# A graph network on one core: row gathers held to fourteen rows ahead of the scan

## The reference

```
xi = x @ W_pre[:Fin];  xj = x @ W_pre[Fin:]
h  = xi[dst] + xj[src] + b_pre
mean, mean_sq = segment_sum(h, dst) / deg, segment_sum(h * h, dst) / deg
std = sqrt(relu(mean_sq - mean * mean) + 1e-5)
mx, mn = segment_max(h, dst), segment_min(h, dst)
agg = concat(mean, mx, mn, std)
out = concat(x, agg, agg * log(deg + 1) / avg, agg * avg / log(deg + 1)) @ W_post + b_post
out = out @ W_lin + b_lin
```

## Time and profile before

| | |
|---|---|
| median of 3 runs | 2161.73 us (2159.77 to 2167.29) |
| the profiled execution | 2173.5 us, of which the span from first to last instruction is 2171.8 us |
| busy in that span | PE 68%, PE weight loads 48%, VectorE 66%, ScalarE 23%, GpSimd 37% |
| mean granted TensorE clock | 0.85 of full speed |
| the gather of layer 0, first to finish | 649.2 to 1302.6 us |
| the gather of layer 1, first to finish | 1413.1 to 2050.8 us |
| row gathers | 688, of 0.947 us each on GpSimd (median) |

### The profile page before, as it was taken

How to read it: one execution, slowest core, us unless ns; L and a number is a source line. 1 busy time by engine, 2 the same in 40 slices (tenths; PEclk the granted TensorE clock), 3 DMA queues, 4 the chain that set the end, 5 groups by cost and what they waited for, 6 DMA issues and landing times.

```text
span 2171.8 us, 30279 instructions
## 1 busy us (share of the span) xinstructions
PE 1475.0 (68%) x11250; PEld 1050.9 (48%) x11250; DVE 1424.4 (66%) x2879; ACT 502.8 (23%) x1074; POOL 808.6 (37%) x831
## 2 busy tenths in 40 slices
PE   0267777767964677777787774656876786687563
PEld 0167766656952445445454552424544554455432
DVE  7899999692065666556665652786755675565457
ACT  3366777300031011111111110221111111111101
POOL 4400000032006545546555514075554555545230
PEclk9878999887986888889898886978898998888877
DMA  5323333333412455455555542145554565554320
GB/s 116 91 107 151 136 137 150 127 114 123 163 63 80 157 181 179 160 177 187 173 184 185 168 152 92 43 135 167 178 172 153 195 197 162 184 168 163 134 70 24
DMA packets 126240, 309.36 MB, mean 142 GB/s; under 512 B 21745, under 2 KB 73409, under 8 KB 125743
## 3 DMA queue, kind: packets, MB, share of 16 engines
q1 hardware_dynamic: 75216, 145.00, 19.0%
q10 hardware_dynamic: 23470, 105.20, 13.9%
q0 software_dynamic: 27440, 57.77, 9.9%
HBM read 167.18 MB, written 140.75 MB: 142 GB/s over the span
## 4 chain that ended last, share of the span: by engine, by line
PE 33%; DVE 32%; another core or an unknown queue 14%; issue 12%; DMA 4%; ACT 2%; POOL 2%; ACTq 1%; DVEq 0%; POOLq 0%
PE ps L1156 16%; PE ps L1284 6%; DVE accs L2159 5%; DVE scanned L2188 3%; DVE accs L2141 3%; DVE scanned L1700 3%; DVE scanned L1697 3%; DVE scanned L1706 3%; PE ps L1296 2%; DMA A<-counts 2%; PE ps L1181 2%; PE ps L1450 1%; PE ps L1385 1%; DVE S L1673 1%
## 5 line engine op out<-in xcount | busy, mean ns | idle before, releaser
L1095 POOL DMA_INDIRECT scanned<-table,rest_idx x688 | 678.5, 986 | 763.0 <-DMA rest_history<-scanned 255.8
L1156 PE MATMUL ps<-big,A 125*128 125x128 bf16 (+1 forms) x7500 | 764.7, 258 | 83.0 <-issue 60.1
L1156 PEld LDWEIGHTS ps<-big,A 125*128 125x128 bf16 x7500 | 622.6, 103 | 226.0 <-issue 118.0
L1284 PE MATMUL ps<-S,big 126*128 126x500 bf16 (+1 forms) x1050 | 281.3, 412 | 254.1 <-DVE accs L2159 163.2
L2159 DVE TENSOR_TENSOR accs<-accs,ps 128x1000 f32<-128x1000 f32 (+1 forms) x154 | 166.9, 1084 | 391.1 <-remote 301.6
L2188 DVE SCALAR_TENSOR_TENSOR scanned<-scanned,rest_neg 128x256 f32<-128x256 f32 x688 | 332.0, 483 | 32.9 <-ACT scanned L905 5.5
L1284 PEld LDWEIGHTS ps<-S,big 126*128 126x128 bf16 x1050 | 101.9, 107 | 375.8 <-DVE accs L2159 179.5
L2141 DVE TENSOR_TENSOR accs<-accs,ps 128x1000 f32<-128x1000 f32 (+1 forms) x154 | 166.0, 1078 | 1.8 <-DVE MS L1814 1.1
L1181 PE MATMUL ps<-scanned 128*128 128x150 bf16 x1050 | 115.7, 252 | 75.6 <-DVE scanned L1706 74.5
L1113 POOL IOTA Y<- 128x784 int32 x1 | 0.8, 787 | 361.7 <-DVEq L1962 361.7
L1181 PEld LDWEIGHTS ps<-scanned 128*128 128x128 bf16 x1050 | 87.2, 132 | 92.6 <-issue 75.6
(11 more groups left out here) (384 smaller groups left out, 1421.7 us busy)
## 6 DMA issues: line engine op xcount, KB each, us to landing
rest_history<-scanned SPq DMA_DIRECT2D x172, 512.0 KB
A<-counts ACTq DMA_DIRECT2D x75, 800.0 KB
S<-picks SPq DMA_DIRECT2D x60, 640.0 KB
picks<-S ACTq DMA_DIRECT2D x25, 800.0 KB
counts<-A ACTq DMA_DIRECT2D x25, 800.0 KB
scanned<-table,rest_idx POOLq DMA_INDIRECT x688
table<-Y SPq DMA_DIRECT2D x10, 320.0 KB, 2.6
S<-picks SPq DMA_DIRECT2D x10, 160.0 KB
```

What stands on the lines that cost most here:

```text
L1095: nc.gpsimd.indirect_dma_start(out=lanes[:, r, s, 0:F], out_offset=None, in_=tables[1 + l], in_offset=bass.IndirectOffsetOnAxis(ap=rest_id ...
L1156: m = nc.tensor.matmul(acc[:, bank, 0:width], A[0:NB, slot, a, :], XS[0:NB, a, c, 0:width], start=a == 0 and c == 0, stop=a == NT - 1 and ...
L1284: m = nc.tensor.matmul(ps[:, bank + h, 0:len(blocks) * NB], XS[0:NB + 1, a, c, 0:F], pick[0:NB + 1, part % RING, 0:len(blocks), a % PART, ...
```

## The change

One constant is new, and each row's gather gets one more wait. Row `i` of a layer is asked for only when VectorE has scanned row `i - 14` of that layer; rows 0 to 13 stay without it. The waits ahead of a batch stay as they are.

```diff
 LANES_RING = 6
+ROWS_LEAD = 14
 ROUND = 1.5 * 2.0 ** 23
...
                         pool.wait_ge(main.scan_ops, BATCH * (n - LANES_RING + 1) + 1)
                     for s in range(BATCH):
                         i = k * BATCH + s
+                        if i >= ROWS_LEAD:
+                            pool.wait_ge(main.scan_ops, l * REST + i + 1 - ROWS_LEAD)
                         nc.gpsimd.indirect_dma_start(
                             out=lanes[:, r, s, 0:F], out_offset=None, in_=tables[1 + l],
                             in_offset=bass.IndirectOffsetOnAxis(ap=rest_idx[:, i:i + 1], axis=0))\
```

## The result

| | before | after |
|---|---|---|
| median | 2164.51 us (2159.77 to 2169.99) | 2095.10 us (2089.68 to 2103.08) |
| the profiled execution | 2173.5 us, span 2171.8 | 2097.7 us, span 2095.9 |

The ratio is 0.9681, with a 95% interval of 0.9639 to 0.9724: **3.2% faster**. Forecast were 2055 us and a range of 1980 to 2175. The sign and the range are right, the size is two thirds of the one forecast: 69 us for 106.

What follows compares the result with a forecast made beforehand. The prediction took VectorE's waits for TensorE's signal, kept up by long gather runs, to bound the stretches. Stalls -94, clock -18 and late rows +6 gave -106 us, so 2055 us from a median of 2161.7, range 1980 to 2175.

Steps and rivals of the forecast that it cites:

- What bounds it: Gather stretches: set by waiting; VectorE's 51 remote waits for TensorE's signal, 329.8 us, caused by long gather runs.
- (1): GpSimd's row gathers: distance ahead of the scan becomes 13 for every row, from 19 up to 22.
- (2): VectorE's stalls in the gather stretches: mean length falls from 6.5 to 4.3 us, bounds 2.6 and 6.4.
- (3): VectorE's stalls in the gather stretches: 55 for 51, 236 us against 330, so 94 us less.
- the formula behind it: Gather stretches: stall length = gathers that GpSimd may still ask for x 1.25 us + 2.6 us.
- (4): TensorE's clock: shorter stalls mostly end before it falls, 18 us less, bounds 0 and 52.
- (5): GpSimd's added wait instruction on each gather: costs 0, other bound 66 us if nothing hides it.
- (6): A batch's last row, gather to negation to scan: late rows cost 3 us a layer, 6 us more.
- Another cause: Rival, chance 0.09: TensorE stops by itself, the 51 stalls stay, time 2162 us within 6.
- More stalls: Rival, chance 0.13: GpSimd never rests long enough, 96 stalls, 413 us, +83, so 2245 us.
- break-even: Count of 4.3 us stalls in the gather stretches at which nothing is gained: 77.
- All but vanish: Rival, chance 0.08: any gap between gathers breaks a run, 12 stalls of 4 us left, about 1850 us.

Runs made afterwards that it cites:

- e10: Kernel before without row gathers after the first 24 rows of layer 0, on a chip with stalls: 1809.6 us against 2153.3, ratio 0.839.
- e2: Kernel before, row gathers after the first 24 rows bringing 128 lines of 64 bytes in place of 512: 1769.7 us against 1767.9, ratio 1.001.
- e7: Kernel after with a distance of 18 rows in place of 14: 1768.1 us, ratio 1.001 to the kernel before on that chip.
- e4: Kernel after with a distance of 10 rows in place of 14: 1888.8 us, ratio 1.069 to the kernel before on that chip.
- e12: Kernel before, a batch's second row asked for only when the batch ahead has landed: 2078.3 us against 2128.1, ratio 0.980.
- e9: Kernel before, a batch's first row asked for only when all four rows ahead have landed: 2245.9 us against 2153.3, ratio 1.041.

## Why the prediction held, and where it was off

**What bounds it: right in place, half right in kind.** VectorE's remote waits were the thing to touch, they come while gathers run, and in the stretches they are gone without the row gathers (e10). "TensorE itself is what stands still" is one half of it: TensorE does slow down with no wait shown (221 products for 642 in 40 us). The other half I missed: in the stall above the signal was due at once and came 7.5 us late, to two engines at the same moment. Which of the two brings the other is open. And one condition was missing that no row of one chip could show: of five chips, three stall and two don't.

**(1) The distance: right.** GpSimd's idle time names the scan, not the store.

**(2) and (3) Length and number: right.** 54 stalls of 4.6 us, for 55 of 4.3: 249 us against 236, and 80.8 saved against 94. The stretches are 612 and 599 us, where I had said near 590. But the formula behind it does not hold, so that the mean came out near is in part luck. I had read that stalls end 2.1 to 3.1 us after the run's last gather. So do 19 of the 26 waits over 6 us of the kernel before, but few of the shorter ones, and in the kernel after only about a quarter: its stalls end 0.0 to 2.7 us behind a gather's end. And from distance 14 to 12 they got no shorter.

**(4) Clock: the step furthest off.** I had stalls of 4.3 us end mostly before the clock falls, and took 18 us for it, on top of the waits. S less the held time is 938.8 us after and 938.6 before: outside the waits nothing came. The clock still falls, as short stretches of the kernel after behind a stall of 6.4 us show (columns as in the earlier trace rows):

```profile
941.00:945.00 4.00, 3.48 (x11) 1.61 (x12) 3.75 (x8) 0.83 (x2) 0.73 (x1) 0.50 0.00 0
946.00:950.00 4.00, 4.00 (x30) 2.93 (x29) 3.68 (x8) 0.86 (x2) 3.08 (x4) 1.00 0.74 211
```

At 0.50 TensorE does 11 products in 4 us, at 1.00 it does 30. But VectorE is busy 3.75 us of the slow four and 3.68 of the fast: TensorE's slower products were not what it waited for at this place. The same is seen over whole stretches. Those of the kernel before on chip 10:

```profile
622.00:1098.00 476.00, 422.95 (x2819) 289.63 (x2816) 401.66 (x697) 99.64 (x248) 346.75 (x343) 0.96 0.68 225
1190.00:1672.00 482.00, 421.85 (x2822) 289.05 (x2822) 405.90 (x700) 102.08 (x252) 347.77 (x344) 0.95 0.67 222
```

The clock is 0.95 to 0.96 there and 0.85 to 0.88 on the first chip, TensorE's products take 845 us in place of 947, and S less the held time is within 12 us (938.6 against 926.5 to 937.9 in e2, e7 and this run). Outside the stalls I had priced a resource where it isn't the bound.

One part stays open. "Held" takes a wait whole. By the modelled end of the lift, some 27 of the 330 us before lie ahead of that end and only 10 of the 249 after. In these TensorE was not done yet, and whether the clock or the crawl made it late, the traces don't say. So up to 17 us of the 80.8 saved may be the term that I had called clock.

**(5) The wait instruction: right, 0.** A distance of 18 adds as many waits as 14 but four for each layer, and its ratio is 1.001 (0.998 to 1.004).

**(6) Late rows: inside its bounds, priced on the wrong chain.** I had forecast 6 us with bounds of 0 to 16. On the first chip the 0.2 us above is what (4) and (6) come to together; on chip 10 the change costs 13 us, of which the profiled S shows none. ScalarE's wait for landings went from 53 to 257 us, and on the first chip it lay beside the stalls. On chip 10 no stall covers it, and at a distance of 10 it is 110 us of S. The chain that I priced, gather to negation to scan, is not the one that pays (17.0 us in e4): it is ScalarE's order, take_sums and loads behind the negation. I had named it and given it nothing.

So the sum was -94 - 18 + 6 = -106, and the profiled executions show -80.8 for the held time, +0.2 for the rest of S and +4.7 outside it, -75.9 in all. The waits gave 13 us less than forecast, and the clock 18 less as a term of its own.

**The rivals.** *Another cause* falls with e10. The Trainium skill, "SBUF — State Buffer", section "Who interferes with whom", says that DMA never contends with a compute engine. By its words the gathers could not cost TensorE's followers 330 us; the measurement decides, 344 us less without them. No trace shows an access to SBUF that waits, so the rule may be true of the ports and yet no ground for the forecast of 2162. *More stalls* didn't come: 54, far from the 77 of break-even. *All but vanish* by "any gap is enough" is refuted twice: the gaps that the change brings left 54 stalls, and those of e12 left 34.

On the pause of e9: the Trainium skill, "DMA: Bandwidth & Descriptors", section "Anatomy of one DMA — SWDGE (gpsimd) path", gives some 2.0 us fixed for one such transfer. An estimate by that page is 3 x 1.25 + 2.0, some 5.8 us for a batch, below my 5.9 to 6.3. The trace has 2.5 us from the start of the gather (741.44) to the start of the negation that waits for it (743.97), and 0.7 more to the next gather, so 7.0 for the batch; that last step neither the page nor I had in the sum.

## What to carry to other kernels

When two engines that wait for different signals of a third start at the same instant, long after the third's work for them by the profile, neither of the two waits is explained by that work; look at what else is going on, here a run of gathers from GpSimd, and at whether the third crawls with no wait shown. A change that treats such a stall is worth what the stall is worth on the chip where it was measured: repeat it on others, with the kernel before beside it, since here the same edit gives 3.2% on one chip and costs 0.8% on another. And price the wait that you add by who stands behind it in the same engine's order, not by the one that it is meant for.

## What the runs showed of the hardware that I had not expected

- The kernel before takes 2164.5, 2153.3 and 2128.1 us on three chips and 1767.9 and 1767.1 on two others, 20% less. On the first chip some 330 us of this are VectorE's waits for late signals of TensorE during row gathers, and 66 lie outside the stretches, in three places with other runs of gathers.
- On the first kind of chip VectorE waited up to 13.9 us for such a signal. On the second kind no signal was late, with over 250 gathers in one run. Why chips differ was not found.
- While 28 gathers went out on the first chip, 25 of them of 4-byte lines, TensorE did 221 products in 40 us at a granted clock of 0.61; on chip 10 it did 642 at 1.00.
- With at most four gathers in a run and pauses of 1.7 us or more between runs, no signal was held in 172 batches (e9, chip 2); with longer runs, 34 were (e12, chip 14).
- 128 lines of 64 bytes took as long as 128 lines of 512, on a chip without stalls: ratio 1.001.
- Apart from the stalls, stretches with a granted clock of 0.85 to 0.88 took at most 12 us longer in some 930 than those with 0.95 to 0.96, while VectorE's busy time was the same (812.6 against 807.6 us).
